# A one-core adaLN block with a scan and a gated expert sum: the second modulated state kept as two fp32r parts, its shift moved into biases

## What is computed

```python
mod = (silu(c) @ wmod).reshape(8, 6, 1, 128)       # sa, ca, ga, sb, cb, gb
ga, gb = sign(ga) * max(|ga|, 0.25), sign(gb) * max(|gb|, 0.25)
h = layernorm(x) * (1 + ca) + sa
v, gate = split(h @ W_in + b_in)
y = sigmoid(gate) * scan(v)            # s[t] = sigmoid(A) * s[t-1] + v[t], times C
x = x + ga * (y @ W_out + b_out)
h = layernorm(x) * (1 + cb) + sb
w = softmax(h @ gate_w + gate_b); w = w * (w >= 0.1); w = w / sum(w)
x = x + gb * sum_e w[:, e] * (h @ expert_w[e] + expert_b[e])
```

## Time and profile before

| | us |
|---|---|
| median of 3 runs | 230.83 |
| the 3 runs | 226.45, 230.83, 231.16 |
| the profiled execution | 228.16 |
| its span | 226.4 |
| TensorE busy | 204.2 |
| VectorE busy | 211.0 |
| ScalarE busy | 171.4 |
| GpSimd busy | 149.5 |

### The profile page before, as it was taken

One profiled execution on the slowest core, in us unless ns is written; L12 is line 12 of the kernel. 1 busy time (PEld: TensorE's weight loads), 2 busy tenths in 40 slices (PEclk: granted clock), 3 DMA queues, 4 the chain that ended last, 5 costly groups with the idle time before them and its releaser, 6 DMA issues.

```text
span 226.4 us, 4220 instructions
## 1 busy us (share of the span) xinstructions
PE 204.2 (90%) x969; PEld 145.8 (64%) x969; DVE 211.0 (93%) x805; ACT 171.4 (76%) x546; POOL 149.5 (66%) x234
## 2 busy tenths in 40 slices
PE   0978869999999999999999999999999999989921
PEld 0863456868677777767686858585858685856700
DVE  5976799988999999999999999999999999998995
ACT  2332154989988889989898989898889799899910
POOL 8250055769586959697877869686868595766900
PEclk9999999999999999999999999999999999999985
DMA  6610011101103020201111111111010101001003
GB/s 210 150 35 0 0 47 49 42 8 51 46 2 91 4 88 6 63 30 51 46 48 48 49 48 46 46 49 48 1 46 3 46 0 48 4 1 46 19 28 93
DMA packets 19233, 9.82 MB, mean 43 GB/s; under 512 B 1305, under 2 KB 19082, under 8 KB 19210
## 3 DMA queue, kind: packets, MB, share of 16 engines
q1 hardware_dynamic: 17536, 9.03, 13.4%
q10 hardware_dynamic: 1674, 0.54, 0.9%
HBM read 5.37 MB, written 4.19 MB: 42 GB/s over the span
## 4 chain that ended last, share of the span: by engine, by line
PE 83%; DVE 7%; ACT 2%; issue 1%; DVEq 0%
PE ring L1520 14%; PE ring L1521 12%; PE ring L1522 12%; PE bank_g L1460 7%; PE bank_b L1503 7%; PE bank_v L1448 7%; PE bank_a L1479 6%; PE bank_b L1423 3%; PE bank_v L1449 3%; PE bank_a L1423 3%; DVE z L903 2%; PE bank_a L1481 2%; PE bank_b L1501 2%; PE bank_v L1544 1%; PE ring L1417 1%
## 5 line engine op out<-in xcount | busy, mean ns | idle before, releaser
L593 ACT ACTIVATE z<-ring,wts 128x128 f32<-128x128 f32 x436 | 121.8, 392 | 7.2 <-DVE wts L891 4.7
L443 POOL TENSOR_TENSOR z<-z 128x512 f32<-128x512 f32 x45 | 60.1, 1347 | 7.7 <-ACT z L593 7.7
L1520 PE MATMUL ring<-expert_w_hi,h_hi 128*128 128x512 f32 x128 | 62.0, 484 | 1.9 <-DVE z L903 0.7
L1522 PE MATMUL ring<-expert_w_hi,h_lo 128*128 128x512 f32 x128 | 50.5, 394 | 0.0
L1521 PE MATMUL ring<-expert_w_lo,h_hi 128*128 128x512 f32 x128 | 50.4, 394 | 0.0
L422 POOL TENSOR_SCALAR xn<-x,neg_mean,rstd 128x128 f32<-128x128 f32 x60 | 26.5, 455 | 33.2 <-DVE rstd L848 33.2
L411 POOL TENSOR_SCALAR xn<-x_in,neg_mean,rstd 128x128 f32<-128x128 f32 x56 | 25.0, 459 | 16.3 <-DVE rstd L848 16.3
L1520 PEld LDWEIGHTS ring<-expert_w_hi,h_hi 128*128 128x128 f32 x128 | 24.2, 189 | 14.4 <-issue 11.1
L964 DVE TENSOR_REDUCE mix<-z 128x256 f32<-128x1024 f32 x15 | 29.7, 1979 | 0.4 <-POOL z L443 0.4
L1521 PEld LDWEIGHTS ring<-expert_w_lo,h_hi 128*128 128x128 f32 x128 | 24.3, 190 | 5.5 <-issue 2.9
L1522 PEld LDWEIGHTS ring<-expert_w_hi,h_lo 128*128 128x128 f32 x128 | 24.1, 188 | 5.7
(11 more groups left out here) (122 smaller groups left out, 362.7 us busy)
## 6 DMA issues: line engine op xcount, KB each, us to landing
x_in<-in_L_attn_x_dram SPq DMA_DIRECT2D x16, 256.0 KB, 2.8
out_dram<-x SPq DMA_DIRECT2D x15, 256.0 KB, 2.3
expert_w<-in_L_ffn_expert_w_dram ACTq DMA_DIRECT2D x2, 256.0 KB, 3.3
wmod<-in_L_wmod_dram SPq DMA_DIRECT2D x1, 384.0 KB, 3.7
out_dram<-x SPq DMA_DIRECT2D x2, 128.0 KB, 1.9
expert_b<-in_L_ffn_expert_b_dram SPq DMA_DIRECT2D x12, 4.0 KB
w_in<-in_L_attn_W_in_dram SPq DMA_DIRECT2D x1, 128.0 KB, 3.9
w_out<-in_L_attn_W_out_dram SPq DMA_DIRECT2D x1, 64.0 KB, 3.6
```

The costliest lines, as they stand in the source:

```text
L443: nc.gpsimd.tensor_tensor(z[:, g % 2, t, 0:4, :], z[:, g % 2, t, 0:4, :], z[:, g % 2, t, 4:8, :], ALU.add).then_inc(folded[t], 1)
L593: last = nc.scalar.activation(z[:, g % 2, t, e, :], bank_k[:, (e % 4) * P:(e % 4 + 1) * P], ACT.Copy, scale=wts[:, g % 2, t, e:e + 1])
L1520: mm(bank_k[:, :], hi, expert_w_hi[:, cols], start=True, stop=False)
L1522: mm(bank_k[:, :], lo, expert_w_hi[:, cols], start=False, stop=True).then_inc(e_ready[k], 1)
```

## The change

- `h2` is gone. `h2_high` writes only scale times the transposed state, rounded to fp32r, and `low_part` takes the difference directly from the bank (`scalar_tensor_tensor`).
- `logits` uses the two parts: 12 products of 8 columns in fp32r in place of 4 in fp32 (8 passes). The shift `sb` times `gate_w` and times the experts' weights is added to the biases: `bias_rows` on TensorE makes it for all batches ahead of the loop, VectorE adds and splits it, and the experts' bias table, now one per batch, goes through DRAM (`spread_expert_bias` on SyncE, two writes and 12 reads).
- The bias operands that had 33 or 40 rows have 96 (`ROWS`).
- `second_norm` moves from GpSimd to ScalarE, as scale and bias (`shifts` on VectorE makes the bias) with its own place in ScalarE's order. Group 0 keeps VectorE's.
- `sum_fours` is replaced by `add_pairs` on GpSimd and `sum_pairs` on VectorE for tiles 2 and 3 too.
- `bank_b` is gone: `turn_xn2` and `logits` use `bank_g`, `turn_parts` uses `bank_v`, and the freed bank holds operands of VectorE's small steps. `root` has one step more.
- In the last group ScalarE weighs six halves and VectorE two, and GpSimd folds tiles 0 and 2.
- Loads are issued from other queues, `pick`, the identity products and `gate_rows` change place and count, and every engine's order is new.

The diff, cut (some 1,800 lines in all; most of the rest are new orders ahead of and behind the loops):

```diff
-LAST_DVE_HALVES = (1, 3, 5, 7)
...
-HALF_ORDER = ((1, -1), (7, -1), (3, 0), (5, 0), (0, 0), (4, 0), (2, 0), (6, 0))
+LAST_DVE_HALVES = (3, 7)
+LAST_DVE_PAIRS = (0, 1)
...
+HALF_ORDER = ((7, -1), (3, 0), (6, 0), (2, 0), (1, 0), (4, 0), (5, 0), (0, 1))
...
 PART = 32
+ROWS = 3 * PART
...
+        scratch = bank("scratch")
...
+        mean_var = scratch_cols(0, 4 * TILES).rearrange("p (c k) -> p c k", k=2)
...
+        near_b = scratch_cols(8 * TILES, 2 * TILES)
...
+            def load_expert_bias():
...
+            def spread_expert_bias():
+
+                sp.wait_ge(bias_high_ready, 1)
+                sp.dma_start(b_hi_d, expert_b_hi[:, :].bitcast(F32)).then_inc(bias_written, 16)
+                sp.wait_ge(bias_low_ready, 1)
+                sp.dma_start(b_lo_d, expert_b_lo[:, :].bitcast(F32)).then_inc(bias_written, 16)
+                sp.wait_ge(bias_written, 16 * 2)
+                sp.wait_ge(zeroed[2], batches)
+                for part, rows in enumerate((b_hi_d, b_hi_d, b_lo_d)):
+                    for t in range(TILES):
+                        r = part * TE + t * experts
+                        sp.dma_start(expert_b_parts[r:r + experts, :, t * P:(t + 1) * P].bitcast(F32),
+                                     rows.rearrange("b (e n) -> e b n", e=experts)).then_inc(bias_in, 16)
...
+            load_vectors()
...
-            sp.wait_ge(x_loaded[1], 16)
-            sp.wait_ge(zeroed[2], 1)
-            for part in range(3):
...
+                nc.scalar.activation(h2_hi[:, g % 2, :], bank_g[:, :], ACT.Copy, scale=mod(3, g)).then_inc(h2_ready, 1)
...
-                nc.scalar.copy(w_parts_t[:, g % 2, :], bank_g[0:3 * TE, 0:P]).then_inc(wt_copied, 1)
...
+            def second_norm(g):
+
+                act.wait_ge(shift_ready, g)
+                for j in range(TILES):
+                    last = nc.scalar.activation(
+                        tile(xn2, g % 2, j), tile(x1, g % SLOTS, j), ACT.Identity,
+                        bias=shift[:, g % 2, j:j + 1], scale=rstd[:, g % 2, j:j + 1])
+                last.then_inc(xn2_ready, 1)
...
-            for s in range(2, 12):
+            gate(4)
+            for s in range(3, 13):
+                weigh(s - 1, 0)
+                second_norm(s)
+                weigh(s - 1, 3)
+                h2_high(s)
+                weigh(s - 1, 6)
+                parts_out(s - 2)
+                weigh(s - 1, 1)
                 weigh(s - 1, 2)
+                h1(s + 2)
                 exponentials(s)
-                weigh(s - 1, 6)
-                h1(s + 2)
-                weigh(s - 1, 1)
-                parts_out(s - 1)
-                weigh(s, 3)
+                weigh(s - 1, 4)
+                weigh(s - 1, 5)
                 gate(s + 2)
-                weigh(s, 5)
-                h2_high(s + 1)
-                weigh(s, 0)
-                h2(s + 1)
-                weigh(s, 4)
-            weigh(11, 2)
-            exponentials(12)
-            weigh(11, 6)
-            h1(14)
+            weigh(12, 0)
+            second_norm(13)
+            weigh(12, 3)
...
-                    vec.tensor_tensor(near_one[:, :], guess_v[:, :], guess[:, :], ALU.mult) \
+                    vec.tensor_tensor(near_a[:, :], guess_v[:, :], guess[:, :], ALU.mult)
+                elif n == 4:
+                    vec.tensor_tensor(near_b[:, :], guess_v[:, :], guess[:, :], ALU.mult) \
                         .then_inc(root_step, 1)
...
-                dve.wait_ge(h2_made, g + 1)
+                b = g // per_batch
                 dve.wait_ge(h2_ready, g + 1)
-                vec.tensor_tensor(h2_lo[:, g % 2, :], h2_t[:, g % 2, :],
-                                  h2_hi[:, g % 2, :].bitcast(F32), ALU.subtract).then_inc(h2_split, 1)
+                vec.scalar_tensor_tensor(out=h2_lo[:, g % 2, :], in0=bank_g[:, :], scalar=mod_cols[:, 3, b:b + 1],
+                                         in1=h2_hi[:, g % 2, :].bitcast(F32), op0=ALU.mult,
+                                         op1=ALU.subtract).then_inc(h2_split, 1)
...
+            def shifts(g):
+                dve.wait_ge(rstd_ready, g + 3)
+                vec.scalar_tensor_tensor(out=shift[:, g % 2, :], in0=mean_var[:, 0:TILES, 0], scalar=-1.0,
+                                         in1=rstd[:, g % 2, 0:TILES], op0=ALU.mult,
+                                         op1=ALU.mult).then_inc(shift_ready, 1)
...
             for s in range(2, 11):
-                root(s + 1, 2)
-                weigh_onto(s - 1, 7, 0)
-                root(s + 1, 3)
-                router(s, 5)
-                root(s + 1, 4)
-                root(s + 1, 5)
-                negated_mean(s + 1)
-                root(s + 1, 6)
-                router(s, 6)
-                root(s + 1, 7)
-                router(s, 7)
+                scan(s + 2)
+                gated(s + 2)
+                x_stats(s + 5, 0)
                 weigh_onto(s - 1, 7, 1)
                 weigh_onto(s - 1, 7, 2)
-                scan(s + 2)
+                x_stats(s + 4, 1)
                 weigh_onto(s - 1, 7, 3)
-                x_stats(s + 5, 0)
-                x_stats(s + 5, 1)
-                gated(s + 2)
-                sum_fours(s - 1, 1)
-                x_stats(s + 5, 2)
+                sum_pairs(s - 1, 0)
+                x_stats(s + 4, 2)
+                x_stats(s + 4, 3)
+                low_part(s + 1)
                 first_residual(s + 2)
-                x_stats(s + 5, 3)
+                sum_pairs(s - 1, 1)
                 x1_stats(s + 2)
-                sum_pairs(s - 1, 0)
-                low_part(s + 1)
                 router(s + 1, 0)
+                moments(s + 2)
+                router(s + 1, 1)
+                root(s + 2, 0)
                 add_bias(s - 1)
-                router(s + 1, 1)
+                root(s + 2, 1)
                 times_gb(s - 1)
-                moments(s + 2)
+                root(s + 2, 2)
                 router(s + 1, 2)
                 result(s - 1)
-                root(s + 2, 0)
+                root(s + 2, 3)
+                root(s + 2, 4)
                 router(s + 1, 3)
-                root(s + 2, 1)
+                root(s + 2, 5)
                 router(s + 1, 4)
-            root(12, 2)
-            weigh_onto(10, 7, 0)
-            root(12, 3)
-            router(11, 5)
-            root(12, 4)
-            root(12, 5)
-            negated_mean(12)
-            root(12, 6)
-            router(11, 6)
-            root(12, 7)
-            router(11, 7)
+                root(s + 2, 7)
+                router(s + 1, 5)
+                root(s + 2, 6)
+                router(s + 1, 6)
+                negated_mean(s + 2)
+                root(s + 2, 8)
...
+            def bias_rows():
+
+                pe.wait_ge(mod_ready, 1)
+                pe.wait_ge(late_in, 16 * 3)
+                pe.wait_ge(gb_ready, 1)
+                mm(ring[0][0:batches, 0:experts], mod_cols[:, 2, :], gate_w[:, :], start=True, stop=True)
+                for h in range(2):
+                    last = mm(ring[2 + h][0:batches, :], mod_cols[:, 2, :], expert_w[:, h * 512:(h + 1) * 512],
+                              start=True, stop=True)
+                last.then_inc(bias_rows_done, 1)
...
+            def logits(g):
+                bank_x = bank_g
                 if g == 0:
...
-                mm(bank_b[:, 0:TE], ones[:, 0:P], gate_b_parts[:, :], start=True, stop=False)
+                    pe.wait_ge(gate_low_ready, 1)
+                pe.wait_ge(h2_split, g + 1)
+                mm(bank_x[:, 0:TE], pick[:, g // per_batch, :], gate_b_parts[:, :], start=True, stop=False)
                 for j in range(TILES):
-                    last = mm(bank_b[:, j * experts:(j + 1) * experts], tile(h2_t, g % 2, j),
-                              gate_w[:, :], start=False, stop=(j == TILES - 1))
+                    cols = bank_x[:, j * experts:(j + 1) * experts]
+                    mm(cols, tile(h2_hi, g % 2, j), gate_w_hi[:, :], start=False, stop=False)
+                    mm(cols, tile(h2_hi, g % 2, j), gate_w_lo[:, :], start=False, stop=False)
+                    last = mm(cols, tile(h2_lo, g % 2, j), gate_w_hi[:, :], start=False, stop=(j == TILES - 1))
...
+            def turn_parts(g):
...
-                mm(bank_v[:, :], w_parts_t[:, g % 2, :], expert_b_parts[:, :], start=True,
+                mm(bank_v[:, :], w_parts_t[:, g % 2, :], expert_b_parts[:, g // per_batch, :], start=True,
...
+            keep_clock(ring[0], 3)
             turn_silu()
+            keep_clock(ring[0], 4)
             modulation_rows()
             modulation_columns()
-            keep_clock(ring[0], 8)
+            keep_clock(ring[0], 24)
+            gate_rows()
             turn_xn1(0)
-            gate_rows()
+            keep_clock(bank_v, 7)
+            state_input(0)
             gate_input(0)
-            state_input(0)
+            after_turn(0)
+            keep_clock(bank_a, 8)
             turn_xn1(1)
```

(97 more changed lines are left out.)

897 lines of the change are left out of this document (465 added, 432 removed), and 3 rows, old and new, of the table LAST_HALVES.

## The result

| | before | after |
|---|---|---|
| median, us (4 runs each) | 228.64 (226.31 to 231.16) | 232.07 (230.92 to 232.86) |
| ratio, 95% interval | | 1.0195 [1.014, 1.025] |
| profiled execution: time, span | 228.16, 226.4 | 232.78, 230.9 |
| first expert half starts | 37.82 | 44.72 |
| state input of group 4 / of group 14 starts | 60.10 / 178.15 | 68.71 / 184.76 |

The change made the kernel about 2% slower, where 225.2 us was forecast. That forecast was 2.4% under the median of three runs, 230.83; with the fourth run the median before is 228.64, and 225.2 is 1.5% under it. The two spans differ by 4.5 us, and the state input's starts split that: up to group 4 the changed kernel is 8.6 us later, over the ten periods behind it gains 2.0 (118.05 against 116.05), and from group 14 to the end 2.1 (48.25 against 46.14). The loop and the end gained; the start lost more than both together gave.

A forecast was written before the change was run, and what follows sets the result against it. TensorE and VectorE were taken as full, TensorE's own pace plus about 0.15 us of waiting giving 11.80. Some 13.5 periods at -0.31 are -4.2; start +2.2 and end -1.0 leave -3.0, hence 225.2 us, range 219.5 to 232.

The forecast's parts named there:

- The start: Ahead of the loop: first expert half at about 40 us instead of 37.8, +2.2 us, bounds -2 and +5.
- State bias, -0.37 a period: TensorE in the loop: with 96 rows for 33 the gaps around the bias product go, -0.37 us, bounds 0 and -0.37.
- Logits, +0.21: TensorE in the loop: 12 products and the bias at 0.115 us cost 1.50 instead of 1.29, +0.21, upper bound +0.46.
- TensorE's wait on VectorE, -0.15: Loop: with VectorE down to about 10.5 us a period, TensorE's 0.15 us wait for a ring bank goes.
- The wait at the second turn: Loop: three halves (2.1 us) barely cover scan and gated; waits of 0.1 to 0.2 us, hence 11.5 rather than 11.35.
- signs of being right: Period 11.4 to 11.6, bias product 0.24, VectorE idle about 1 us, ScalarE above 95%, first half at 39 to 41.
- ScalarE, 11.1: Loop: second_norm adds 1.4 us, h2 and its bias go; ScalarE busy 11.1 of 11.5 us (10.7 to 11.3), still fits.
- VectorE 10.5 and GpSimd 8.7: Loop: busy time per period falls to about 10.5 us on VectorE from 11.8, and 8.7 on GpSimd from 9.2.
- The bias table, 0: Start: reads land at 58.5 us, mixed_bias(0) comes at 58.8; priced 0, 2 us late would be 2 us lost.
- The end, -1.0: Behind the last product: VectorE's chain -2.1 us, ScalarE's extra halves and norms +1.1, together -1.0.
- The start is longer: Rival, together with a late bias table: 2 to 4 us more, time 227 to 229, chance 0.20.
- the rivals: ScalarE paces loop, 239, 0.10; rows don't matter, 233.6, 0.10; table late or start longer, 0.20; start no longer, 221, 0.20.

The follow-up runs named there:

- a_early: The changed kernel with GpSimd's clears of the bias table and expert_low ahead of first_norm(2): 225.66 us, ratio 0.988 to the kernel before.
- a_bank: The changed kernel with gate_b_rows, the held cast's source, in the scratch PSUM bank, GpSimd's order unchanged: 223.89 us, ratio 0.980 to the kernel before.
- a_more: The changed kernel with GpSimd's clears 6 and 7 moved ahead of first_norm(3), so GpSimd works longer without a pause: 235.25 us, one run.
- a_clock: The changed kernel, cast still held, with 16 more idle TensorE products ahead of logits(0): 228.99 us, ratio 1.001 to the kernel before.
- k_idle8: a_bank with 8 instead of 24 idle products behind the modulation: median 223.98 us, ratio 0.984 to the kernel before, one execution of 310.26 apart.
- k_log8: a_bank without four of the logits' products per group (state's low part with gate weights' high part): 218.68 us, ratio 0.963 to the kernel before.

## Why the prediction failed, step by step

**The start** is the step that failed: "`gate_bias` on VectorE in front of `low_part(0)` (1.2)", together with "the seven more clears ... lie ahead of the loop ...; no price". Each was priced as if the other weren't there. The clears and `expert_low` keep GpSimd busy without a pause exactly when VectorE's cast comes, and the cast cost 3.95 and not about 0.2. The experiments show that as cause from both sides: it goes when GpSimd is done earlier (a_early) or when the source is in PSUM (a_bank), and grows by as much as GpSimd's row of work grows (a_more). The clears took 0.52 each, not "about 1.1". What was missed besides is the second half of the bill: 3.74 us of idle TensorE was followed by 1.2 GHz until about 47 us, another 3.4 us (a_clock). The two make 7.3 us, and the changed kernel without them has a span of 223.6, where the sum gave 223.4.

The trace of the kernel before had the same thing in small. Its VectorE and GpSimd, not among the rows above:

```profile
34.54 0.15 DVE L811 BATCH_NORM_AGGREGATE mean_var<-bn 128x2 f32<-128x6 f32 x1
34.72 0.69 DVE L821 TENSOR_SCALAR var_e<-mean_var 128x8 f32<-128x8 f32 x1
```

```profile
33.03 2.35 POOL L401 TENSOR_TENSOR expert_w_lo<-expert_w,expert_w_hi 128x1024 fp32r<-128x1024 f32 x1
```

An operation on 128x8 takes 0.69 and ends when `expert_low` does (35.4), between others of 0.15 to 0.18.

That the rest of the start's sum seems right is partly luck: "+2.2" was asked for at the first half, and without the stall it was +0.1 (37.95 against 37.82), with another +1.1 up to the state of group 4, which the sum did not have. The 24 idle products ran from 8.39 to 16.24, close to the "16.8" assumed, and against k_idle8 16 of them account for 3.4 us of it.

**State bias, -0.37 a period:** right in size. The gap went, and came back by 0.39 when the rows went back to 33. The Trainium skill (TensorEngine Tiling (Array Packing)) has row tiling up to 64 contracted rows (When to Use Tiling) and a change of mode drain TensorE (Key Properties); both runs agree with it.

**Logits, +0.21:** they take 1.36 (twelve loads at 0.111, and 0.03 for the bias product), where 1.50 was taken: +0.07. The loads set the price, as said; k_log8 gives 0.111 each once more.

**TensorE's wait on VectorE, -0.15:** went, as said. These three give 11.80 - 0.37 + 0.07 - 0.15 = 11.35, and the measured period less its wait is 11.31. The prediction's own sum gave 11.49 with no new wait in it, and the waits that it expected had no term: that 11.5 came near 11.61 is in part because the logits were priced 0.14 too high.

**The wait at the second turn:** "waits of 0.1 to 0.2 us" were expected with "next to nothing left over" of the cover. It is 0.30: `scan`, 1.28, starts 0.20 behind the state's last product, `gated` ends at 130.11, and the turn starts 2.50 us behind the state's last product where three halves and the turn of the parts cover 2.20. So 11.61 instead of 11.5. Ten periods gained 2.0 us where 3.1 were forecast. Of the signs of being right, the period, the bias product at 0.24, VectorE's idle 0.87 us and ScalarE at 95% came; the first half at 39 to 41 didn't.

**ScalarE, 11.1:** 11.05, and it doesn't pace the loop. For `second_norm` 0.35 each were taken; the timeline gives 0.385:

```profile
128.52 1.66 ACT L648 ACTIVATE xn<-x,shift,rstd 128x128 f32<-128x128 f32 x4
130.06 1.15 ACT L635 ACTIVATE z<-ring,wts 128x128 f32<-128x128 f32 x4
```

(130.06 - 128.52) / 4. By the Trainium skill's dearer operand from SBUF (VectorE: DVE Perf Modes, on the TRN2 errata) the estimate was 0.17 a period more than 1.4, and measured is +0.14; the total did not follow, since other terms came out smaller.

**VectorE 10.5 and GpSimd 8.7:** 10.74 and 8.56.

**The bias table, 0:** right. `mixed_bias(0)` shows no wait on a transfer in the changed kernel, where the stall made it late (65.44). In a_bank it comes at 55.11, earlier than the 58.8 of the prediction, and shows none either.

**The end, -1.0:** right in size for the stretch that it priced, by other terms. From the last product's columns (221.77 + 0.24) to VectorE's end (228.40) are 6.4 us, against 7.4 before: -1.0, where -2.1 were taken for VectorE's chain and +1.1 for ScalarE (the figures given for ScalarE, 2.0 + 2.1 - 2.7, make 1.4). Another 0.95 came between the last two states (10.94 against 11.89 us), which the sum had only as a period's 0.31.

```profile
221.77 0.40 PE L1604 MATMUL ring<-expert_w_hi,h_lo 128*128 128x512 f32 x1
...
227.65 0.75 DVE L1071 TENSOR_TENSOR x<-bank_v,x 128x256 f32<-128x256 f32 x2
```

The end has a hold as well, in the changed kernel, a_early and a_bank alike. One `sum_pairs` of the last group, with both sources in SBUF, takes 1.5 us where the others take 0.41, beside a GpSimd addition. VectorE's and GpSimd's rows of the changed kernel:

```profile
218.91 1.51 DVE L1018 TENSOR_TENSOR mix<-z 128x256 f32<-128x256 f32 x1
```

```profile
218.86 1.27 POOL L486 TENSOR_TENSOR z<-z 128x512 f32<-128x512 f32 x1
220.07 0.44 POOL L468 CAST w_parts<-wts 128x64 fp32r<-128x64 f32 x1
```

The prediction had no term for it. What its 1.1 us cost at the end no run shows.

**The chances.** The mechanism that decided was in none of the rivals. "The start is longer" had a range of 2 to 4 us and named no cause but the bias table; a held VectorE with a fall of the clock behind it is 7.3.

## What to carry to other kernels

Before a small VectorE operation from SBUF to SBUF is put into the chain of the start, look at what GpSimd does at that moment: 0.2 us of copying lasted as long as GpSimd had work without a pause, 3.95 us, and TensorE's idle time behind it was paid almost a second time at the lower clock. A source in PSUM (one line here) took the changed kernel from 232.1 to 223.9, 2.0% below the kernel before [1.0 to 3.0%]; its profiled execution, at 222.77, was one with the early clock. And a gap taken from one engine is worth only what the next wait leaves of it: the same 0.37 us were worth 0 in the kernel before, 0.07 in the changed one.

## What the runs showed of the hardware

- A VectorE cast with source and target in SBUF, begun while GpSimd works, ended within 0.03 us of the end of GpSimd's whole row of instructions: 3.95, 3.96 and 4.88 us for 8x32 elements, 0.17 alone. The row held the end of the norms, clears and a subtraction, one right behind the other. With the source in PSUM it took 0.18 beside the same work.
- Not every VectorE operation from SBUF to SBUF is held. The second to fourth operation of `second_norm(0)` (L1091, 128x128, 31.24 to 32.09) took 0.34 each beside GpSimd's norms, as long as the first, which began ahead of them, and in a_bank four `x1_stats` (L851, 30.27) took 0.87 together beside GpSimd's clear and subtraction.
- Nor does a hold always last for the whole row. `sum_pairs` (L1018, 218.91) ended at 220.42, 0.3 us behind the GpSimd addition that it had met, though GpSimd went on at once; GpSimd's next cast then took 0.44 where it takes 0.24 otherwise.
- The Trainium skill (SBUF — State Buffer, "SBUF: two separate sides") has an exclusive lock for VectorE operations in a mode with two ports, or with two inputs in SBUF against a GpSimd operation that reads SBUF; whoever starts first gets it "for the whole instruction". `sum_pairs` agrees with that. The held cast agrees with a lock, but it wasn't handed over between GpSimd's instructions, only when GpSimd had none left. Why it differs from `sum_pairs` these runs don't show.
- TensorE, idle for 3.74 us (35.0 to 38.75), ran at 1.2 GHz behind it and was back at 2.4 GHz at about 47 us; with idle products in those 3.7 us the granted clock stayed at 1.00.
- A product of 33 rows between two of 128 costs 0.37 to 0.39 us in all; for one of 96 rows no gap shows beyond its columns.
